# A vision tower on one core: Gelu's late low parts behind the product spectrum, the intake's turn behind four down blocks, GpSimd's last two residues behind x2's low part

## What is computed

```python
h = _L0_tok_ref(x, L0_tok_W)                       # patches @ W
h = h + _L0_attn_ref(_layernorm(h), ...)
h = h + _L0_ffn_ref(_layernorm(h), ...)

def _L0_attn_ref(x, in_w, in_b, mod_w1, mod_b1, mod_w2, mod_b2, kernel, out_w, out_b):
    x_proj = x @ in_w + in_b
    h = jax.nn.gelu(x @ mod_w1 + mod_b1, approximate=False)
    mod = h @ mod_w2 + mod_b2
    modulated = x_proj * mod
    x_fft = jnp.fft.rfft(modulated.transpose(0, 2, 1), n=Lx)
    k_fft = jnp.fft.rfft(kernel, n=Lx)
    y = jnp.fft.irfft(x_fft * k_fft[None], n=Lx).transpose(0, 2, 1)
    return y @ out_w + out_b

def _L0_ffn_ref(x, ...):
    base_out = x @ base_W.T + base_b
    shared_out = (x @ shared_A.T) @ shared_B.T
    gate = softmax(x @ router_W.T + router_b)      # six experts, the top two kept, made to sum to 1
    routed_out = sum over experts of gate_e * (x @ routed_A_e.T) @ routed_B_e.T
    return base_out + shared_out + routed_out
```

## Time and profile before

| | before |
|---|---|
| median of 3 runs | 1333.79 us (1330.24 to 1340.2) |
| profiled execution, its time | 1336.16 us |
| profiled execution, its span | 1334.4 us |
| mean granted TensorE clock | 0.973 |
| TensorE busy (matmul / weight load) | 1249.8 / 1182.5 us, 94% / 89% |
| VectorE busy | 972.9 us, 73% |
| ScalarE busy | 696.6 us, 52% |
| GpSimd busy | 424.3 us, 32% |
| mean share of the DMA engines | under 25% |

### The profile page before, as it was taken

One profiled execution on the slowest core, in us unless ns is written; L12 is line 12 of the kernel. 1 busy time (PEld: TensorE's weight loads), 2 busy tenths in 40 slices (PEclk: granted clock), 3 DMA queues, 4 the chain that ended last, 5 costly groups with the idle time before them and its releaser, 6 DMA issues.

```text
span 1334.4 us, 20338 instructions
## 1 busy us (share of the span) xinstructions
PE 1249.8 (94%) x7734; PEld 1182.5 (89%) x7734; DVE 972.9 (73%) x2321; ACT 696.6 (52%) x1287; POOL 424.3 (32%) x459
## 2 busy tenths in 40 slices
PE   9989999999999999999999999999999999999998
PEld 8888988989889988898898898898898888988996
DVE  5578777777777777777777777876767877678777
ACT  6645555544556445554446564545554455645442
POOL 3433233232333232232323332323323232333130
PEclk9999999999999999999999999999999999999999
DMA  7221123221222212322112232112222123221100
GB/s 233 83 63 33 56 76 75 64 42 51 70 76 75 64 25 63 76 75 64 33 55 75 76 75 64 32 56 76 75 64 48 51 66 76 66 74 32 27 21 32
DMA packets 132128, 84.76 MB, mean 64 GB/s; under 512 B 111815, under 2 KB 125998, under 8 KB 128190
## 3 DMA queue, kind: packets, MB, share of 16 engines
q1 hardware_dynamic: 132030, 83.46, 23.6%
HBM read 43.07 MB, written 12.85 MB: 42 GB/s over the span
## 4 chain that ended last, share of the span: by engine, by line
DVE 37%; PE 29%; ACT 18%; DMA 8%; issue 7%; ACTq 0%; DVEq 0%
DMA prod<-spec_y 8%; ACT gelu L674 6%; DVE gelu_l L1100 6%; PE rows_ps L1464 6%; PE turn L1742 5%; ACT gelu_h L679 5%; PE rows_ps L1466 5%; PE rows_ps L1465 5%; DVE x_l L1184 4%; ACT L674 3%; DVE bn L968 2%; DVE norm L1015 2%; DVE spec_y L1140 2%; PE rotating L1464 1%; DVE h_sb L1166 1%
## 5 line engine op out<-in xcount | busy, mean ns | idle before, releaser
L525 POOL TENSOR_TENSOR patches_l<-patches,patches_h 128x384 fp32r<-128x384 f32 (+1 forms) x186 | 190.0, 1044 | 309.3 <-ACT patches_h L626 309.3
L530 POOL TENSOR_TENSOR gelu_l<-gelu,gelu_h 128x784 fp32r<-128x784 f32 x62 | 115.9, 1891 | 333.8 <-ACT gelu_h L679 327.9
L1464 PE MATMUL rotating<-x_h,w_h 128*128 128x392 f32 x512 | 180.3, 352 | 0.5 <-ACT x_proj L663 0.4
L1464 PE MATMUL rotating<-gelu_h,w_h 128*128 128x392 f32 x512 | 177.9, 347 | 0.0
L1464 PE MATMUL rows_ps<-tokw_h,patches_h 128*128 128x256 f32 x570 | 176.7, 310 | 0.5 <-DVE patches_l L897 0.5
L1465 PE MATMUL rotating<-x_l,w_h 128*128 128x392 f32 x512 | 174.5, 341 | 0.0
L1466 PE MATMUL rotating<-x_h,w_l 128*128 128x392 f32 x512 | 174.4, 341 | 0.0
L1465 PE MATMUL rotating<-gelu_l,w_h 128*128 128x392 f32 x512 | 174.3, 340 | 0.0
L1466 PE MATMUL rotating<-gelu_h,w_l 128*128 128x392 f32 x512 | 174.1, 340 | 0.0
L1465 PE MATMUL rows_ps<-tokw_l,patches_h 128*128 128x256 f32 x570 | 172.6, 303 | 0.0
L1466 PE MATMUL rows_ps<-tokw_h,patches_l 128*128 128x256 f32 x570 | 171.3, 300 | 0.0
(11 more groups left out here) (294 smaller groups left out, 3138.1 us busy)
## 6 DMA issues: line engine op xcount, KB each, us to landing
patches<-dram_x_rest SPq DMA_DIRECT2D x30, 1152.0 KB, 5.5
out<-h_sb SPq DMA_DIRECT2D x30, 384.0 KB, 2.5
prod<-spec_y SPq DMA_TRANSPOSE x90, 3.1
patches<-dram_x_first SPq DMA_DIRECT2D x2, 384.0 KB, 5.9
h_sb<-dram_x_second SPq DMA_DIRECT2D x1, 768.0 KB, 7.7
patches<-dram_x_fourth SPq DMA_DIRECT2D x1, 768.0 KB, 8.5
h_sb<-dram_first SPq DMA_DIRECT2D x2, 320.0 KB, 3.2
gelu<-dram_w SPq DMA_DIRECT2D x1, 512.0 KB, 8.0
```

The costliest lines, as they stand in the source:

```text
L525: pool.tensor_tensor(patches_l[:, k, 0:n], patches[:, k, 0:n], patches_h[:, k, 0:n].bitcast(F32), ALU.subtract).then_inc(pool_patches_lo, 1)
L530: pool.tensor_tensor(gelu_l[:, 2 * j:2 * j + 2, :], gelu[:, 2 * j:2 * j + 2, :], gelu_h[:, 2 * j:2 * j + 2, :].bitcast(F32), ALU.subtract)\
L1464: pe.matmul(ps, w_h, x_h, start=first, stop=False, skip_group_check=onto_read)
```

## The change

Three places. On VectorE both late Gelu subtractions of a round stand behind the product spectrum; before, one stood ahead of it. On TensorE the turn of the intake's normalised rows stands behind four blocks of the second half of `mlp_down` and no longer behind five. On GpSimd the residues 4 and 5 of the patches stand behind the second fold and behind a new wait, for both halves of x2's low part of this round; before, residue 4 stood ahead of that fold and residue 5 behind it, without the wait.

```diff
-TURN_AT = 5
+TURN_AT = 4
...
                 fold(mid, 0)
                 if i + 2 < ROUNDS:
-                    patches_lo(i + 2, (3, 4))
+                    patches_lo(i + 2, (3,))
                 fold(mid, 1)
                 if i + 2 < ROUNDS:
-                    patches_lo(i + 2, (5,))
+                    if i >= 2:
+                        pool.wait_ge(dve_x2_lo, DH * (i - 1))
+                    patches_lo(i + 2, (4, 5))
...
                 if in_range(tail):
                     finish(tail, rows_ps)
-                for j in range(0 if i == 1 else 2, 3):
-                    gelu_lo(mid, j)
                 if in_range(back):
                     real_products(back)
                     imaginary_products(back)
                     spectrum_of_y(back)
-                gelu_lo(mid, 3)
+                for j in range(0 if i == 1 else 2, 4):
+                    gelu_lo(mid, j)
                 if in_range(back):
                     whole_y(back)
                     y_lo(back)
```

## The result

The changed kernel takes 1226.54 us (median of 4 runs, 1224.82 to 1228.1) where the kernel before takes 1336.2 beside it (median of 4, 1330.24 to 1340.2): a ratio of 0.918, 95% interval 0.914 to 0.922. In a later set, beside three other kernels, it took 1226.68 (median of 6) against 1340.76 (median of 11): 0.915 (0.9125 to 0.9175). The forecast was 1233, with a range of 1222 to 1264. It was taken off the profiled execution of the kernel before, 1336.2 us; the profiled one of the changed kernel took 1228.1, 108 us less where the forecast's terms make 102.5.

A forecast was written before the change was run, and what follows sets the result against it. TensorE, busy 94%, was taken as the bound, through its waits and clock. Terms of 46.5 (inverse's wait), 31 (clock) and 25 us (low parts) sum to 102.5, from 1336.2 to about 1233 us; range 1222 to 1264.

The forecast's parts named there:

- The clock: TensorE's drops to 1.2 GHz after the gap before the inverse transform vanish in all 20 slow rounds: 31 us.
- The rival that the drops stay: About as many rounds still fall to the 1.2 GHz level, so 31 us stay: 1264 us, chance 0.12.
- The inverse's wait: TensorE's inverse transform no longer waits for VectorE's late product spectrum: 1.55 us a round, 30 rounds, 46.5 us.
- X1's and x2's low parts: TensorE's waits before projection and routing shrink, routing products start sooner: 0.85 us in 29 rounds, 25 us.
- neither edit alone would give it: Routing's 0.8 to 1.0 us gain needs both turn and GpSimd edits, since each chain binds about as late.
- The join and the fold: GpSimd's second fold, moved up, meets VectorE's joining copy; the copy loses 0.1 us, 1.0 at most.
- the rival that the fold eats the gain: VectorE's joining copy loses most of a microsecond to GpSimd's fold, x2's chain gains nothing: about 1255 us, chance 0.07.
- The rivals of y: Two cases where y's low part comes late and the mixer waits: 1248 us, chance 0.10; 1364 us, chance 0.02.
- The slack: Time between y's low part being finished and the mixer's start, forecast as 0.2 us and kept after the change.
- the 1248: The whole y comes later, y's slack is overdrawn by half a microsecond, the mixer waits: 15 us, chance 0.10.
- the slower case: Both late Gelu subtractions held up 1.74 us each, y 3.5 us late, mixer waits 3.3 us: 1364 us, chance 0.02.

## Why the prediction was right, and where it was off

**The clock, 31 us forecast.** Right in cause and size. Filling the gap without removing the wait gave 31 us by the profiled spans and 34 by the medians. The rival that the drops stay is out: 1.00 in every round of each kernel without the gap or with half of it, and drops in every kernel that kept it whole.

**The inverse's wait, 46.5 us forecast at 1.55 a round.** The mechanism stands: the products start 0.03 us behind the forward transform and are not held up by GpSimd's subtraction, as 0.69 us at 584.85 shows; none of the 116 products in the rounds took over 0.69. The Trainium skill, "SBUF — State Buffer", section "SBUF: two separate sides", has VectorE take the pair that it shares with GpSimd only for operations with two SBUF inputs or in a two-port mode; the trace agrees. The term was too small. A round at full clock goes from 39.55 us (39.62 with the gap filled) to 37.8 with the Gelu edit alone: 1.75, 52.5 us in 30 rounds, and the 6 us missing are all of the distance by the profiled executions (108 measured, 102.5 forecast) and most of that from 1233 to 1226.5. I had bounded the term by the idle time of the row, 1.45, and of the weight loads, 1.7, and taken a value between. The idle time counts from the modelled end of the last matmul, 0.28 us after its start, but the next one in a row of such matmuls starts after 0.12: 0.16 us of what looks busy is gap. The embedding's last two matmuls ahead of the wait that ends at 603.08:

```profile
601.24 0.28 PE L1465 MATMUL rows_ps<-tokw_l,patches_h 128*128 128x256 f32 x1
601.36 0.27 PE L1466 MATMUL rows_ps<-tokw_h,patches_l 128*128 128x256 f32 x1
```

The inverse transform itself is 0.1 us shorter when it does not start from rest (1.93 against 2.03 at full clock). Together 1.71. The bound from the weight loads (51.6 us in 31, 1.66) was the nearer one.

**X1's and x2's low parts, 25 us forecast at 0.85 a round.** The sum is right, 0.86 (37.89 to 37.03), but how it is shared between the two edits was not foreseen. x2's low part takes 1.03 us in all 29 rounds, as read from the one undisturbed round. The step that failed is the sentence that neither edit alone would give it. GpSimd's edit alone gives 0.65 of it, the turn alone nothing, and the turn behind GpSimd's edit the last 0.2. The two chains are not equally late: at 625.49 x2's was last by 0.36 + 0.16 = 0.52 us although TensorE had already been made late by x1's, and by 0.63 in the mean (14.2 us in 30, and the same 0.16), which is what GpSimd's edit alone gives. I had set the wait for x2's low part in that row (0.36) beside the one for x1's (0.43) as if they were the slack of two chains, but the second is what is left of one chain after the other has already made TensorE late.

**The join and the fold.** The second fold does meet VectorE's joining copy, and in the frequent round the loss falls on GpSimd:

```profile
568.43 0.59 POOL L545 TENSOR_TENSOR folded<-modulated 128x196 f32<-128x196 f32 x1 [0.34 <-DVE modulated L1114]
568.91 1.06 DVE L1181 COPY norm<-prod 128x1536 uint16<-128x1536 uint16 x1 [0.56 <-DMA prod<-spec_y]
568.97 1.03 POOL L546 COPY folded<-modulated 128x2 f32<-128x2 f32 x1
...
570.78 1.03 DVE L1186 TENSOR_TENSOR x_l<-norm,x_h 128x384 fp32r<-128x384 f32 x2 [0.81 <-ACT x_h L729]
571.89 2.00 POOL L525 TENSOR_TENSOR patches_l<-patches,patches_h 128x384 fp32r<-128x384 f32 x2 [1.35 <-DVE x_l L1186]
```

A copy of two elements lasts 1.03 us on GpSimd, because it stands behind VectorE's. In the round at 478 to 515 the DMA lands 0.4 us later, the fold's last piece is already running, and then it is VectorE that stands still:

```profile
494.99 0.60 POOL L547 TENSOR_TENSOR folded<-modulated 128x196 f32<-128x196 f32 x1
...
495.16 1.35 DVE L1181 COPY norm<-prod 128x1536 uint16<-128x1536 uint16 x1 [0.93 <-DMA prod<-spec_y]
```

That round is of the 37.3 us kind. In all eight of them the copy starts 1.47 to 1.81 us behind the second modulation and not 1.2, because the DMA lands later, and then takes 1.09 to 1.44 us instead of 1.06. So the rival that the fold eats the gain is a small truth: the long rounds lose 0.45 us each, the later DMA is the greater part of the delay in seven of the eight, and the hold by the fold 0.03 to 0.4 us of it. Why the DMA lands later in those was not tried.

**The sum.** 1336.2 - 102.5 is 1233.7, not the 1233.5 that was rounded to 1233; it changes nothing. That the total came out within 7 us is no luck of terms that cancel: each was within 6 us of what its own run gave.

**The rivals of y.** The mixer does not wait. The slack is 0.4 us and the two subtractions are not held up, so neither the 1248 nor the slower case had its condition.

## What to carry to other kernels

Read a regular gap on TensorE twice: once as the wait, and once for the clock that may drop behind it, which here was 31 to 34 us on 52, and nothing when the gap was half as long. Useless matmuls in the gap are a cheap test that tells the two apart. And where VectorE and GpSimd share a stretch, let the operation that nobody waits for wait for the one that TensorE waits for, by a semaphore: a mere change of order made it worse.

## What the runs showed of the hardware

- TensorE fell to the 1.2 GHz level after a gap of 1.45 us in 20 of 29 rounds, after one of 0.7 to 0.8 us in none, and never after the two gaps of 0.43 and 0.36 us that lie 5 us apart.
- In the undo of the Gelu edit alone the same gap, in rounds 1 us shorter, cost a drop in 15 of 29 rounds instead of 20. With GpSimd's edit alone, in rounds 0.65 us shorter, it was 20 again. Why some rounds are spared was not tried.
- Where a GpSimd and a VectorE operation on SBUF alone met, one ran its usual time and the other ended only behind it. VectorE's Gelu subtraction lasted 2.71 us for 0.97 and ended 0.84 us behind GpSimd's (1.87 us); GpSimd's two-element copy lasted 1.03 us for 0.19 and ended 0.03 us behind VectorE's copy (1.06 us). A VectorE product with one input in PSUM ran beside GpSimd at its usual 0.69 us.
